# Feed forward in pairs of units, with gates by broadcast transfer instead of by matmul, and weights asked for later

## The reference

```
x = x + attn_a(layernorm(x))   # 16 heads, two softmax maps per head of 4 channels each:
                               #   o = a1 - lambda * a2, rms norm over 8 values, projection
x = x + ffn(layernorm(x))
x = x + attn_b(layernorm(x))   # head by head energies summed over tokens (16 x 16), projection
x = x + ffn(layernorm(x))

ffn(x): shared = silu(x @ Ws_up) @ Ws_down                 # 128 -> 64 -> 128
        aff = x @ centroids.T; top 8 of 64 by aff + bias
        cw[t, e] = sigmoid(aff) / sum over the chosen, else 0
        routed = sum over e of cw[t, e] * (silu(x @ W_up[e]) @ W_down[e])   # 64 experts, 64 wide
        shared + routed
```

## Time and profile before

| | us |
|---|---|
| median of 3 runs | 1249.27 (1243.14 to 1249.95) |
| profiled execution | 1244.09 |
| its span, first to last instruction | 1242.2 |
| busy in the span: TensorE / VectorE / ScalarE / GpSimd | 1124.0 / 1050.7 / 944.1 / 156.0 |
| mean granted TensorE clock | 0.95 of 2.4 GHz |

### The profile page before, as it was taken

How to read it: one execution, slowest core, us unless ns; L and a number is a source line. 1 busy time by engine, 2 the same in 40 slices (tenths; PEclk the granted TensorE clock), 3 DMA queues, 4 the chain that set the end, 5 groups by cost and what they waited for, 6 DMA issues and landing times.

```text
span 1242.2 us, 22561 instructions
## 1 busy us (share of the span) xinstructions
PE 1124.0 (90%) x8256; PEld 576.7 (46%) x8256; DVE 1050.7 (85%) x1584; ACT 944.1 (76%) x1709; POOL 156.0 (13%) x252
## 2 busy tenths in 40 slices
PE   3459999999999999999998899999999999999998
PEld 1202222222222222222222224867887877787886
DVE  3799999999999999999999413888887898788986
ACT  1407889888889888888888867767777767777765
POOL 4273000000000000000000210222020212011000
PEclk9758999999999999999999858999999999999999
DMA  6821110011101110111000000000001000100000
GB/s 183 277 75 44 45 46 20 26 45 46 32 15 45 45 45 4 43 45 45 19 27 20 3 1 1 1 1 1 1 1 34 1 1 1 43 1 10 1 9 9
DMA packets 46397, 40.79 MB, mean 33 GB/s; under 512 B 23184, under 2 KB 32784, under 8 KB 46288
## 3 DMA queue, kind: packets, MB, share of 16 engines
q1 hardware_dynamic: 34816, 34.62, 9.3%
q10 hardware_dynamic: 11472, 4.74, 1.7%
HBM read 28.46 MB, written 10.88 MB: 32 GB/s over the span
## 4 chain that ended last, share of the span: by engine, by line
PE 73%; DVE 12%; ACT 6%; issue 5%; ACTq 1%; POOL 1%; DMA 1%; SPq 1%; DVEq 0%; POOLq 0%
PE PS L1142 21%; PE PS L1124 12%; DVE NEGMAX L879 8%; PE PS L1242 8%; PE PS L1243 8%; PE PS L1244 8%; PE PS L1094 7%; PE PS L1255 4%; ACT PR L688 2%; PE PS L1104 2%; ACT OTS L700 1%; DVE HL L921 1%; PE PS L1035 1%; DVE HF L1012 1%; ACTq L618 1%
## 5 line engine op out<-in xcount | busy, mean ns | idle before, releaser
L688 ACT ACTIVATE PR<-PS 128x512 f32<-128x512 f32 x1024 | 552.5, 596 | 122.6 <-PE PS L1124 110.5
L879 DVE TENSOR_REDUCE NEGMAX<-PS 128x1 f32<-128x1024 f32 x512 | 585.4, 1213 | 22.3 <-PE PS L1094 18.7
L1124 PE MATMUL PS<-QB,KB 32*128 32x512 bf16 x1024 | 308.6, 398 | 37.8 <-ACT OTS L700 34.0
L1142 PE MATMUL PS<-PR,VG 128*32 128x256 f32 (+1 forms) x3840 | 337.3, 425 | 2.7 <-ACT PR L688 2.1
L1012 DVE TENSOR_TENSOR HF<-SI,PS 128x512 f32<-128x512 f32 x256 | 174.6, 683 | 64.5 <-ACT SI L789 63.5
L1094 PE MATMUL PS<-KA,QA 32*128 32x512 bf16 x1024 | 197.4, 407 | 33.7 <-DVE NEGMAX L879 32.1
L789 ACT ACTIVATE SI<-PS 128x512 f32<-128x512 f32 x256 | 152.4, 596 | 80.4 <-PE PS L1244 76.7
L1124 PEld LDWEIGHTS PS<-QB,KB 32*128 32x128 bf16 x1024 | 85.3, 91 | 263.1 <-ACT PR L688 215.7
L771 ACT ACTIVATE HH<-HF 128x512 fp32r<-128x512 f32 x264 | 165.3, 627 | 40.8 <-DVE HF L1012 35.6
L921 DVE TENSOR_TENSOR HL<-HF,HH 128x512 fp32r<-128x512 f32 x264 | 188.5, 714 | 5.8 <-ACT HH L771 5.5
L1142 PEld LDWEIGHTS PS<-PR,VG 128*32 128x32 f32 x3840 | 77.0, 110 | 122.0 <-issue 87.6
(11 more groups left out here) (179 smaller groups left out, 841.8 us busy)
## 6 DMA issues: line engine op xcount, KB each, us to landing
QA<-q_stack SPq DMA_DIRECT2D x64, 128.0 KB, 2.7
KA<-k_stack SPq DMA_DIRECT2D x64, 64.0 KB, 2.4
QB<-q_stack SPq DMA_DIRECT2D x16, 256.0 KB, 2.9
KB<-k_stack SPq DMA_DIRECT2D x16, 256.0 KB, 2.9
q_stack<-PARTS SPq DMA_DIRECT2D x12, 256.0 KB, 3.9
k_stack<-PARTS SPq DMA_DIRECT2D x12, 256.0 KB, 4.0
RAWU<-in_L_ffn_W_up_dram ACTq DMA_DIRECT2D x4, 512.0 KB, 9.6
X<-in_L_attn_a_x_dram SPq DMA_DIRECT2D x4, 256.0 KB, 4.1
```

The source lines that it names most:

```text
L688: nc.scalar.activation(PR[:, s % PRING, r, :], PS[:, SCORE_BANK.get(n, 4 + n % 3), :], ACT.Exp, scale=SCALE_A).then_inc(p_ready, 1)
L879: nc.vector.tensor_reduce(NEGMAX[:, ga % 2, col:col + 1], PS[:, e:e + 2, :].rearrange("p b n -> p (b n)"), axis=AX_X, op=ALU.max, negate=T ...
L1124: mm(PS[:, SCORE_BANK.get(n, 4 + n % 3), :], KB[strip, u, mt * P:(mt + 1) * P], QB[strip, u, half * BANK:(half + 1) * BANK], start=True, s ...
L1142: last = mm(PS[STRIP * r:STRIP * (r + 1), 7, cols], VG[:, u, mt, r // 2, :], PR[:, s % PRING, r, cols], start=mt == 0, stop=mt == TB - 1 a ...
```

## The change

Nothing is computed differently but for the gates, which are multiplied in full float32 from DRAM copies instead of in two parts through a matmul.

- **Steps of two pairs.** A chunk has 17 steps: 16 full ones of two units each (six matmuls up, six down, 1024 columns for every other instruction) and the shared unit alone. There are two places of two banks for `up`, four for HF, HH and HL, and `down` runs three steps behind.
- **Gates.** SEL and its matmul are gone. ScalarE evacuates the transposed gates of a chunk to CWT, SP writes them to DRAM (gate_d) and reads them back, two transfers of 64 partitions by 2 x 512 values a step, into one of three places of GATE.
- **Silu** is written in place in PSUM, and VectorE multiplies PSUM by GATE.
- **ScalarE's order** in a step is side stages, `high` of the step before, silu. **VectorE's** is side stages, `low` of the step before unless GpSimd has it, the product `gated`.
- **Low on GpSimd** in steps where `low_on_pool` says so: 46 of 136.
- **SIDE** is written anew for 17 steps, with three PSUM banks in turn, and separate semaphores for what ScalarE and what VectorE evacuates.
- **Attention b:** one transfer reads back the mixed values instead of 16.
- **Start.** ScalarE issues no transfer before its evacuations. SP issues CENT, WB and, after the first constant rows, the nine small loads. Once batch 0's stacks are written, ScalarE issues KA of group 0 (SP only QA), then RAWD and two quarters of RAWU; the other two quarters behind the copy to WDH. The addition of BPROJ stands behind the first `shift_parts`.

```diff
-UNITS = PAIRS + 1
-LAG = 4
+FULL = PAIRS // 2
+WIDES = FULL + 1
+LAG = 3
 HPLACES = LAG + 1
+ZSLOTS = 2
+GSLOTS = 3
...
+    (1, 2): [("heads_T", 2)], (1, 4): [("proj", 2), ("stats", ("f", 2))], (1, 5): [("y_T", 0), ("stats", ("b", 0))],
+    (1, 6): [("norm", ("f", 2))], (1, 7): [("norm", ("b", 0))], (1, 8): [("x_T", ("f", 2))], (1, 9): [("affinity", 2)],
+    (1, 10): [("heads_T", 3), ("x_T", ("b", 0))], (1, 11): [("top", 2)], (1, 12): [("proj", 3), ("stats", ("f", 3))],
+    (1, 13): [("sum", 2)], (1, 14): [("norm", ("f", 3))], (1, 15): [("gate_T", 2)], (1, 16): [("x_T", ("f", 3))],
+    (2, 0): [("affinity", 3)], (2, 2): [("top", 3)], (2, 4): [("sum", 3)], (2, 6): [("gate_T", 3)],
...
+DVE_SIDE = ("proj", "stats", "norm", "y_T", "out_b", "top", "sum", "rms_sums")
+POOL_SIDE = ("stats", "x_T", "affinity", "top", "sum", "rms_scale")
...
+def low_on_pool(g):
+
+    n, w = divmod(g + 1, WIDES)
+    return works((n, w), DVE_SIDE) and not works((n, w), POOL_SIDE) or not works((n, w), POOL_SIDE) and w % 3 == 0
...
+            write_gates(0)
+            for n in range(2 * NCH):
+                sp.wait_ge(gate_w, 16 * (n + 1))
+                gates = gate_d[n].rearrange("(w u h) t -> w h u t", u=2, h=2)
+                for w in range(FULL):
+                    k = n * FULL + w
+                    if k >= GSLOTS:
+                        sp.wait_ge(hf_ok, k - GSLOTS + 1)
+                    for h in range(2):
+                        sp.dma_start(GATE[E * h:E * (h + 1), k % GSLOTS, :, :],
+                                     gates[w, h].partition_broadcast(E)).then_inc(gate_ld[k % GSLOTS], 16)
...
+                if n < 2 * NCH - 1:
+                    write_gates(n + 1)
...
-            act.wait_ge(qa_ld[0], MAX_LOADS)
-            load_up(2)
-            load_up(3)
+            act.wait_ge(st_w[0], STACK_WRITES)
+            for rp in range(R // 2):
+                for h in range(2):
+                    act.dma_start(KA[2 * STRIP * h:2 * STRIP * (h + 1), 0, rp, :],
+                                  k_stack[0, 2 * rp:2 * rp + 2, :, h * BANK:(h + 1) * BANK].rearrange("r s n -> (r s) n")
+                                  ).then_inc(qa_ld[0], 16)
+            act.dma_start(RAWD[:].rearrange("p (j d) -> p j d", d=DIM),
+                          w_down.rearrange("(j e) f d -> (e f) j d", e=2)).then_inc(ld_exp, 16)
+            load_up(0)
+            load_up(1)
             act.wait_ge(ld_exp, 48)
             for n, (dst, src) in enumerate(((WDH, RAWD), (WUH, RAWU), (WSUH, RAWSU), (WSDH, RAWSD))):
                 if n == 1:
+                    load_up(2)
+                    load_up(3)
                     act.wait_ge(ld_up, 16 * 4)
...
+            for g in range(2 * NCH * WIDES):
+                n, w = divmod(g, WIDES)
+                if n and w == LAG:
+                    chunk_sum(n - 1)
+                side((n, w))
+                if g:
+                    high(g - 1)
+                silu(g)
...
+                nc.vector.tensor_tensor(HF[:, k, :, :], PS[:, z:z + 2, :], GATE[:, h % GSLOTS, :, :], op=ALU.mult).then_inc(hf_ok, 1)
...
+            for g in range(2 * NCH * WIDES):
+                n, w = divmod(g, WIDES)
+                side((n, w))
+                if g and not low_on_pool(g - 1):
+                    low(g - 1)
+                if is_full(g):
+                    gated(g)
...
+            for g in range(2 * NCH * WIDES):
+                n, w = divmod(g, WIDES)
+                side((n, w))
+                if w == 0 and n:
+                    pe.wait_ge(xl_ok, n + 1)
+                if g:
+                    up(g)
+                if g >= LAG:
+                    down(g - LAG)
```

More of the change, by code:

```diff
@@ L134 @@
[L134 to L145, removed]
@@ L146 @@
-for n, b in ((2, 0), (4, 1)):
[L148 to L169, removed]
-SIDE_STEPS = sorted([k for k in SIDE if isinstance(k, int)]) + sorted([k for k in SIDE if not isinstance(k, int)])
-SIDE_ITEM = ring_order([st for k in SIDE_STEPS for st in SIDE[k] if st[0] in (
-    "heads_T", "proj", "x_T", "affinity", "gate_T", "y_T", "gram", "gram_k", "q_k", "energy", "mix_T", "v_mix",
-    "v_all", "out_b")])
+    (0, 1): [("heads_T", 1)], (0, 3): [("proj", 1), ("stats", ("f", 1))], (0, 5): [("norm", ("f", 1))],
@@ new lines, in lows_before @@
+def lows_before(g, pool):
+    return sum(low_on_pool(k) == pool for k in range(g))
+SIDE_STEPS = sorted([k for k in SIDE if isinstance(k, int)]) + sorted([k for k in SIDE if not isinstance(k, int)])
+BY_DVE = ("proj", "y_T", "out_b", "gram", "gram_k", "q_k", "energy", "mix_T", "v_mix")
+BY_ACT = ("heads_T", "x_T", "affinity", "gate_T", "v_all")
+SIDE_ITEMS = [(st, not isinstance(k, int)) for k in SIDE_STEPS for st in SIDE[k] if st[0] in BY_DVE + BY_ACT]
+SIDE_ITEM = ring_order([st for st, _ in SIDE_ITEMS])
@@ L175 @@
+TAIL_ITEMS = sum(not late for _, late in SIDE_ITEMS)
+FREED_DVE = ring_order([st for st, _ in SIDE_ITEMS if st[0] in BY_DVE])
+FREED_ACT = ring_order([st for st, _ in SIDE_ITEMS if st[0] in BY_ACT])
+SIDE_ORDER = [st for st, _ in SIDE_ITEMS]
 LN = ring_order([("a", c) for c in range(NCH)] + [st[1] for k in SIDE_STEPS for st in SIDE[k] if st[0] == "stats"])
@@ L451, in _ @@
+            store(NCH - 1)
             sp.wait_ge(stored, 16 * NCH)
@@ L553, in _, with side @@
                     values((s + 1) % 2, i * 2 + (s + 1))
-            for where in SIDE_STEPS:
-                if where == NQ - 19:
-                    shift_parts(0, NG - 1)
-                for stage, arg in SIDE[where]:
+            def side(where):
+                for stage, arg in SIDE.get(where, ()):
                     if stage == "rms_scale":
@@ L1196, in side @@
                         pe.wait_ge(ch_ok, arg + 1)
-                        last = transposes([CH[:, j, :] for j in range(4)])(bank)
+                        for j in range(4):
+                            last = nc.tensor.transpose(PS[0:E, bank, j * P:(j + 1) * P], CH[:, j, :], ident[:])
                     elif stage == "y_T":
@@ L1290, in _ @@
-            for g in range(2 * NCH * UNITS - LAG, 2 * NCH * UNITS):
+            pe.wait_ge(m_free, len(ITEM))
+            for g in range(2 * NCH * WIDES):
+                n, w = divmod(g, WIDES)
+                side((n, w))
+                if w == 0 and n:
+                    pe.wait_ge(xl_ok, n + 1)
[3 more added lines that the diff above has]
+                    down(g - LAG)
+            for g in range(2 * NCH * WIDES - LAG, 2 * NCH * WIDES):
                 down(g)
```

385 lines of the change are left out of this document (224 added, 161 removed).

## The result

The changed kernel takes 1262.95 us (median of three; 1259.49 to 1265.15) against 1247.6 us before on the same chip: ratio 1.0124, 95% interval 1.0076 to 1.0172. The change makes the kernel 15 us slower, 1.2%, and the interval excludes no change; the forecast was 1261 and "slower". The profiled execution took 1259.49 us.

A forecast was written before the change was run, and what follows sets the result against it. TensorE bounded the kernel before; after the change a serial ring through VectorE and ScalarE would. Feed forward +24 us and start -10 us gave +14 on a middle of 1246.7: 1261 us, range 1236 to 1284.

The forecast's parts named there:

- The cycle: Feed-forward step through VectorE and ScalarE: 3.61 us with low on VectorE, 3.30 us with low on GpSimd.
- chunk end: Feed forward, from step 15's product to the next chunk's first: 4.5 us each, 31.5 us for seven.
- the ring: Feed forward: gated, high and silu follow serially through VectorE and ScalarE, 3.30 or 3.61 us against TensorE's 2.78.
- Side stages: Feed forward: statistics, top, affinity, exponentials and others stick out of the engines' gaps and lengthen the ring by 34.3 us.
- the rival of hidden stages: Feed forward: waits counted in series fall together and the 34 us of side stages vanish: 1227 us; chance 0.21.
- From the last product to the last sum: End of feed forward: the product itself 1.2 us, then high, silu, high, low and matmuls 4.9 us.
- The start: Before attention's first shift: earlier x copy and reordered loads bring the shift to 76 to 81 us, gaining 10 us.
- The sum: Whole kernel: feed forward +24 us, start -10 us, so +14 us and 1261 us.
- TensorE the bound: Rival, feed forward: TensorE stays the bound, 60 + 10 us go, 1177 us; chance 0.06.
- The clock: Rival: TensorE's idling drops its clock; ten drops give 1281 us, kept low throughout 1530 us; chance 0.10.
- GpSimd late or shut out: Rival: GpSimd's side stages push its lows by over 1 us, shutting out VectorE's next low: 1276 us; chance 0.10.
- Gates: Gate loads priced at zero; rival: broadcasts at half pace make a step 5 us, 1440 us; chance 0.05.

The follow-up runs named there:

- both orders: Changed kernel with silu before high on ScalarE and product before low on VectorE: 1221.23 us; also with no low part on GpSimd: 1202.19 us.
- ScalarE's order: Changed kernel with only ScalarE turned, silu before high: 1261.56 and 1259.0 us; also with no low part on GpSimd: 1277.46 us.
- The second start: Kernel with both engines' orders turned and no GpSimd low; RAWD load moved to SyncE's queue, one RAWU quarter instead of two before WDH's copy: 1198.66 us.
- The two single orders: Changed kernel, GpSimd's low parts kept, with one engine's order turned: ScalarE's silu before high 1261.56 us; VectorE's product before low 1276.12 us.
- VectorE's order: Changed kernel with only VectorE turned, product before low: 1276.12 us; also with no low part on GpSimd: 1255.87 us.
- the fastest kernel: Changed kernel with both engines' orders turned, no low part on GpSimd and RAWD's load on SyncE's queue, one RAWU quarter before WDH's copy: 1198.66 us.

## Why the prediction was right, and where it was not

- **The cycle** was right to the hundredth of a microsecond: 3.62 and 3.31 against 3.61 and 3.30, chunk end 4.53 against 4.5. It is shown by the timeline and by the kernel without low parts on GpSimd (+14.0 us of feed forward for a forecast difference of 12.1). That both orders had to change before the ring opened is shown best where GpSimd has no low part: plain steps of 3.62 us with neither or with ScalarE's order, 3.32 with VectorE's, 2.8 with both.
- **Side stages.** First to last product took 484.6 us (forecast 488.9). With the plain steps and ends as forecast, the sides and GpSimd's contention came to about 32 us against 36.3. By kind: statistics with update 0.78 (0.9), top 0.54 (0.6), affinity inside a chunk 1.4 (1.6), at step 16 2.0 (1.9), at step 0 3.2 (3.4), exponential 1.4 (1.4), chunk 0's root steps 1.8 in all (3.3). Only chunk 0's root steps were clearly smaller than counted, so the rival of hidden stages (0.21) is out.
- **From the last product to the last sum** 6.2 us (forecast 1.2 + 4.9).
- **The start** is the step that was wrong in size: "10 us", range 7 to 12, measured 4.4 both at the first up product and, in the kernel before with this start alone, by the ratio. The working had the maxima right (14.2 us earlier) and WDH right (48.15), but put WUH at 60 to 65 us with the RAWU parts landing as before. They landed 18.1 us after their issue (9.6 before), ScalarE's queue stood 14.3 us on the first two and 13.8 on the last two, and all of GpSimd's chain moved with WUH (66.79). The second start, which moves only these loads, has the shift 6 us earlier (75.89).
- **The sum.** Feed forward cost 19.2 us where 24 were forecast, the start gave 4.0 to 4.4 where 10 were: two misses of 5 and 6 us that cancel. That 1261 came within 2 us of 1262.95 is luck to that extent.
- **TensorE the bound** (0.06) is out here, and it is what both reorderings made of the kernel, at 2.8 us a step. **The clock** (0.10): 0.97 in the first stretch, for a drop that the kernel before has too, and 1.00 in all others; out. More drops came only in the reordered kernels. **GpSimd late or shut out** (0.10): 1.3 us instead of the 15 of that rival, and the 2 us put in for it held. The mechanism is real, though, and stretched VectorE's normalising by 20 us as soon as the ring no longer kept VectorE away, 15 us of feed forward net. **Gates** (0.05): no wait for them, and nothing to win without them, though their price of zero rested on a landing of 2.9 us and they took 3.9.
- **The experiments' own forecasts** missed their ranges four times. The two single orders did for one reason: each forecast followed one ring and forgot what the freed engine runs into next (ScalarE's place behind TensorE in the first, VectorE's side work beside GpSimd in the second). Both orders together came out 16 us too high, and GpSimd's low parts account for 15 of them; VectorE's order without them came out 16 too high as well, in its side steps and chunk ends.

What stays open: the side steps of 4 to 6 us in the kernels with one order or both, in full. The norm's groups are settled. In the fastest kernel 18 of the 25 steps of 3.9 us and more inside chunks have VectorE busy for 96% or more (statistics, top), 5 have ScalarE busy for 95% or more (table loads), and TensorE's idle time in feed forward is only 20 us. What single stages cost there, and what low parts that come late for the down products cost, wasn't taken apart.

## What to carry to other kernels

Before halving the instructions of engines that wait for the bounding one, write out, in program order, the ring that leads from one step's instruction to the next step's on each engine: if it holds all of them in series, wider tiles make it longer and the hidden engine becomes the bound. When two in-order engines each hold one link of such a ring, turning one alone opens only the part that runs through it. With GpSimd out of the way ScalarE's order gained nothing, VectorE's 22 us, and both 75 us; with GpSimd's low parts in place each alone gained nothing or lost, and both gained some 42 us. And what one profile of a whole kernel gains or loses may lie in a part that the change didn't touch: compare the stretch that it did. A load moved behind other work must be followed to its landing and to the last engine that works on it, because the first stage to move earlier is seldom the one that waits longest.

## What the hardware showed that I had not expected

- A VectorE SBUF-to-SBUF instruction of 128 columns, 0.34 us alone, took up to 2.45 us beside a GpSimd subtraction of 1024 columns (2.40 us in the changed kernel). It waits out the whole instruction: the one that began at 1126.68 in the kernel with VectorE's order ended at 1129.10, GpSimd's pair of subtractions at 1129.02. VectorE's product with one operand in PSUM kept 1.21 to 1.23 us beside it.
- ScalarE's silu from PSUM to PSUM took 1.01 us for 1024 columns, its copy from SBUF to SBUF 1.06 (a square 1.044 in the earlier trace rows). The quicker PSUM destination of the Trainium skill (ScalarE: Activation LUTs, Step-by-step: what each stage is for) shows in that pair, by 0.05 us, if the two functions cost alike, which no run here separates.
- The issue of one RAWU load held ScalarE's queue for 4.0 to 9.8 us in the changed kernel (four loads, 28.1 us) and for 0.4 to 4.9 us in the second start (9.9 us); that the down weights' load ahead of it is the reason was not separated from the other loads of that time.
- With one attention program, the stretch from the first shift to the first product took 674.6 us at a mean granted clock of 0.95 and 690.0 us at 0.93. What made the clock differ from run to run stays open.
